# Correlation products on two 64-wide column tiles, with the high parts multiplied in one direction only

## The chip, the cores and the metric

One core of a Trainium2 chip. The metric is the device time of one execution in microseconds (us). One profiled execution gives the trace. Engines: PE multiplies matrices, DVE, ACT and POOL work on vectors, SP issues DMAs.

## The reference

Two layers with the same form are applied to x of shape (8, 512, 32, 32). Each normalizes x in 32 groups of 16 channels, correlates every pixel with its 5 x 5 neighbours (dot products over 512 channels of vectors of unit length), appends these 25 numbers to the channels, multiplies by a 512 x 537 matrix, adds a bias, applies relu and adds the result to x:

```python
norm = jnp.sqrt(jnp.sum(feature * feature, axis=1, keepdims=True))
fn = feature / jnp.maximum(norm, EPS)
fp = jnp.pad(fn, ((0, 0), (0, 0), (PAD, PAD), (PAD, PAD)))
sims = []
for cc in range(CS):
    for r in range(CS):
        sims.append(jnp.sum(fp[:, :, r:h + r, cc:w + cc] * fn, axis=1))
vol = jnp.stack(sims, axis=1)
x = jnp.concatenate([feature, vol], axis=1)
out = jnp.einsum('bihw,oi->bohw', x, conv_w) + conv_b[None, :, None, None]
return jax.nn.relu(out)
...
x = x + _L0_conv_ref(_gn(x), L0_conv_conv_w, L0_conv_conv_b)
x = x + _L1_conv_ref(_gn(x), L1_conv_conv_w, L1_conv_conv_b)
```

## The kernel before

A unit is one layer of one image; there are 16, in the order: layer 0 of images 0 to 3, layer 1 of the same, then images 4 to 7. A unit's x is four channel tiles of 128 channels (partitions) by 1024 pixels. The steps of unit u, and who does them:

- Statistics: DVE (`stats_tile`, L759; `stats_done`), PE averages them over groups (`average`, L461), DVE and ACT make scale and shift from that (`unit_affine`, L778 to L802; `deviations`, L621, the square root on ACT).
- Operands: ACT writes the normalized tile in f16, the high part (`norm_tile`, L627). ACT or, for units 0 to 2, POOL writes twice the exact value in f32 into `v2`, two buffers (`double_tile`, L633; `double_tiles`, L432). DVE subtracts twice the high part and so gets twice the low part in f16 (`low_tile`, L808).
- Correlation products (`product`, L470; `products`): the pixels are 8 blocks of 128 (4 image rows). For each block, PE multiplies the block's high part, as 128 weight columns, with high and with twice low of the 8 image rows around it: 256 columns, 192 at the image's edges. Four channel tiles accumulate. Two blocks share one bank of `gram_ps` (512 columns), and there are two banks, so the products of a unit are four steps p, and step p waits until ACT has evicted step p - 2 (`band_out_of_psum`, L643). Twice low, taken in one direction, stands for low in both, since the products of a pixel pair are later added up over both directions and halved.
- The band of products goes to DRAM and comes back skewed, so that each pixel has its neighbours in one row (`band_through_dram`, L340 and L346, on SP). DVE makes the vectors' lengths and scales (`neighbours`, L832 to L852), PE transposes (`turn`, L520), ACT copies the rows out (L654), SP writes them to DRAM (`rows_to_dram`, L356 and L358), POOL (SP for units 0 and 1) reads the shifted views back (`views_from_dram`, L267 to L277), DVE combines them (`correlation`, L817 to L825), and POOL moves the 25 numbers into `vol` (`volume_in`, L286).
- Channel products: 8 groups g of a unit (`channels`, L530), each 12 matmuls of 512 columns into one of four banks of `conv_ps`: high weights by high, low weights by high, and half the high weights (`whh`, made on POOL at L424) by twice low. `volume` (L539) adds the 25 numbers. ACT applies bias and relu (`rectified`, L662), DVE adds into x (`added`, L886).

All engines run their programs in the order in which they are written. From slot k = 3 on, a slot of PE is: products p = 0 and 1 of unit k, `average(k + 1)`, products 2 and 3, then groups 4 to 7 of unit k - 2 and 0 to 3 of unit k - 1, with `turn(k)` before the seventh. ACT evicts p = 0, takes the square root of unit k + 1, evicts p = 1, normalizes a tile of unit k + 1, and evicts p = 2 and 3. In slot 4 the weights of layer 1 are transposed between the groups (L510). SP loads images 4 to 7 in slots 4 and 6 to 8 (`load(TEAM)`, `tiles_in`), ahead of the rows of that slot.

Of the kernel before, what the change touches and what calls it, by code (L numbers as in the profile page):

```python
# [31 lines left out]
P = 128  # L32
# [25 lines left out]
def build(nc, x, w0, b0, w1, b1, out):  # L58
# [10 lines left out]
    BAND = (ROWS + 2 * R) * WI  # L69
    PAIRS = BLOCKS // 2  # L70
    REACH = 2 * R * WI + S
# [21 lines left out]
    GSZ = GPAD + BLOCKS * P * BAND + GPAD  # L93
    GROUPS = 2 * KT
    BN = 6
    assert (B, UNITS) == (BATCHES, B * LAYERS) and BAND * 2 == HALF
# [7 lines left out]
    with ctx:  # L104
# [17 lines left out]
        whh = sb("whh", [P, LAYERS, KT, C], F16)  # L122
# [3 lines left out]
        v2 = sb("v2", [P, 2, PIX], F32)  # L126
        band = sb("band", [P, PAIRS, HALF], F32)
# [19 lines left out]
        affine = sb("affine", [P, 2, 2, KT], F32)  # L147
# [30 lines left out]
        w_half = sem("w_half")  # L178
# [6 lines left out]
        twice = sem("twice")  # L185
        low = sem("low")
        gram = sem("gram")
# [16 lines left out]
        CONSTS = 11  # L204
        BN_STEPS = KT + KT + 2
        GN_STEPS = 11
# [41 lines left out]
        V2_ON_POOL = (0, 1, 2)  # L248
# [51 lines left out]
        def _(sp):  # L300
# [32 lines left out]
            def band_through_dram(k):  # L333

                q = k % 2
                for p in range(PAIRS):
                    sp.wait_ge(band_sb, PAIRS * k + p + 1)
                    dst = bass.AP(band_dram, q * GSZ + GPAD + 2 * p * P * BAND,
                                  [[BAND, P], [P * BAND, 2], [1, BAND]])
                    sp.dma_start(dst, band[:, p, :].rearrange("p (a n) -> p a n", a=2)).then_inc(band_out, 16)  # L340
                sp.wait_ge(band_out, 16 * PAIRS * (k + 1))
                wait(sp, rn_step, RN_STEPS * k)
                for h in range(HALVES):
                    src = bass.AP(band_dram, q * GSZ + GPAD - R + h * FOLD * P * BAND,
                                  [[BAND + 1, P], [P * BAND, FOLD], [1, REACH]])
                    sp.dma_start(skew[:, h:BLOCKS:HALVES, :], src).then_inc(skew_in, 16)  # L346
# [29 lines left out]
            for k in range(STEADY, SLOTS):  # L376
# [3 lines left out]
                tiles_out(k - 2, (2, 3))  # L380
                tiles_in(k - 2)
# [3 lines left out]
                if valid(k):  # L385
                    rows_to_dram(k)
# [5 lines left out]
        def _(pool):  # L392
# [14 lines left out]
            pool.memset(band[:, 0, 0:R * WI], 0.0).then_inc(const_step, 1)  # L407
            pool.memset(band[:, PAIRS - 1, HALF - R * WI:HALF], 0.0).then_inc(const_step, 1)
# [11 lines left out]
            def half_weights(l):  # L420

                for t in range(KT):
                    pool.wait_ge(w_high, W_HIGHS * l + t + 1)
                    pool.tensor_scalar(whh[:, l, t, :], wh[:, l, t, :], 0.5, 1.0, ALU.mult, ALU.mult  # L424
                                       ).then_inc(w_half, 1)

            def double_tiles(u, tiles):

                pool.wait_ge(gn_step, GN_STEPS * (u + 1))
                for t in tiles:  # L430
                    wait(pool, low, KT * u + t - 1)
                    pool.tensor_scalar(v2[:, t % 2, :], xs[:, ring_slot(unit_batch(u)), t, :],  # L432
                                       affine[:, 1, 0, t:t + 1], affine[:, 1, 1, t:t + 1], ALU.mult, ALU.add
                                       ).then_inc(twice, 1)

            double_tiles(0, range(KT))
            scaled_weights(0)
            half_weights(0)
            double_tiles(1, range(KT))
            volume_in(pool, 0)  # L440
            double_tiles(2, range(KT))
            volume_in(pool, 1)
            for k in range(EARLY, UNITS):
                if k == W1_SLOT:
                    half_weights(1)
# [7 lines left out]
        def _(pe):  # L453
# [10 lines left out]
            def product(u, j, t, part):  # L464

                p, h = j // 2, j % 2
                r0 = max(ROWS * j - R, 0)
                r1 = min(ROWS * (j + 1) + R, HI)
                at = h * BAND + (r0 - (ROWS * j - R)) * WI
                return pe.matmul(gram_at(u, p)[:, at:at + (r1 - r0) * WI],  # L470
# [519 lines left out]
```

## Time and profile before

| | |
|---|---|
| timed runs, us | 540.31, 537.4, 541.9 (median 540.31) |
| span of the profiled execution, us | 538.4 (its total is not given apart) |
| PE busy | 490.8 us, 91% of the span, 2824 matmuls |
| DVE, ACT, POOL busy | 350.5 (65%), 278.6 (52%), 131.8 (24%) |
| channel products L530, chain that ended last | 56% of the span |
| correlation products L470, same chain | 14% |
| moved by DMA | 75.81 MB, 141 GB/s |

Matmuls are pipelined: a matmul's duration includes a tail in which the next one already runs, so the distance between two starts, not the duration, is what one costs in a row. PEld is the load of a matmul's weights, which runs beside the matmul before it. A share of the whole span is an average over a start, a steady stretch and an end with different limits.

### The profile page before, as it was taken

The page shows a single profiled execution, that of the slowest core. Times are in us where ns is not written, and L with a number is a line of the kernel's source. Part 1 is how long each engine was busy: PE and PEld are TensorE (multiplying, and loading weights), DVE is VectorE, ACT ScalarE, POOL GpSimd, SP SyncE. Part 2 cuts the span into 40 slices and gives each one's busy share as a digit, 9 for nine tenths or more (in the row PEclk, how much of TensorE's full clock was granted, in tenths as well). Part 3 has the DMA queues.
Part 4 walks back from the last instruction along what each step waited for, and adds up shares of the span by engine and source line. Part 5 has one row for each costly group of instructions (what it writes and reads, how often), then busy time and mean ns, then how long its engine had stood idle before and what let it go on. Part 6 is the DMA issues. An engine that isn't in the chain of part 4 may idle for free.

```text
span 538.4 us, 7705 instructions
## 1 busy us (share of the span) xinstructions
PE 490.8 (91%) x2824; PEld 278.2 (52%) x2824; DVE 350.5 (65%) x820; ACT 278.6 (52%) x370; POOL 131.8 (24%) x189
## 2 busy tenths in 40 slices
PE   0658699489998999999999999999999999999996
PEld 0535355354644646464645556464646455564442
DVE  4788794767869296958758595858677676433322
ACT  1352544575394656647393757556473938433222
POOL 3453511040521313131220404040313112040400
PEclk9989799789999999999999999999999999999999
DMA  8282444441332716494957625042332326362332
GB/s 295 99 270 67 129 165 133 133 134 38 94 92 74 219 49 211 149 309 131 321 165 254 212 102 161 15 129 47 98 89 75 110 79 185 138 203 90 126 126 114
DMA packets 58547, 75.81 MB, mean 141 GB/s; under 512 B 11764, under 2 KB 45612, under 8 KB 58510
## 3 DMA queue, kind: packets, MB, share of 16 engines
q1 hardware_dynamic: 48718, 66.40, 36.7%
q0 software_dynamic: 9792, 8.92, 7.0%
q8 instruction: 22, 0.36, 0.3%
q14 instruction: 15, 0.12, 0.1%
HBM read 34.97 MB, written 37.79 MB: 135 GB/s over the span
## 4 chain that ended last, share of the span: by engine, by line
PE 77%; DVE 10%; ACT 4%; DMA 4%; POOL 2%; SPq 2%; issue 2%; DVEq 0%; ACTq 0%
PE conv_ps L530 56%; PE gram_ps L470 14%; PE conv_ps L539 5%; DVE stats L759 3%; POOL v L432 2%; DVE opnd L808 2%; DMA xs<-in_x_dram 1%; ACT opnd L627 1%; PE turn_ps L520 1%; ACT v L633 1%; DVE wmax L858 1%; ACT act_out L662 1%; DMA skew<-band_dram 1%; DMA band_dram<-band 1%; DVE xs L886 1%
## 5 line engine op out<-in xcount | busy, mean ns | idle before, releaser
L530 PE MATMUL conv_ps<-opnd,wh 128*128 128x512 f16 x512 | 194.9, 381 | 1.2 <-DVE wl L874 1.2
L530 PE MATMUL conv_ps<-opnd,whh 128*128 128x512 f16 x512 | 194.7, 380 | 0.0
L530 PE MATMUL conv_ps<-opnd,wl 128*128 128x512 f16 x512 | 194.7, 380 | 0.0
L662 ACT ACTIVATE act_out<-conv_ps,bias,wdown 128x512 f32<-128x512 f32 x128 | 96.4, 775 | 141.0 <-PE conv_ps L539 129.1
L886 DVE TENSOR_TENSOR xs<-xs,act_out 128x512 f32<-128x512 f32 x128 | 87.7, 696 | 50.8 <-ACT act_out L662 50.2
L470 PE MATMUL gram_ps<-opnd 128*128 128x256 f16 (+1 forms) x960 | 105.0, 269 | 3.4 <-ACT band L643 3.4
L470 PEld LDWEIGHTS gram_ps<-opnd 128*128 128x128 f16 x960 | 91.1, 100 | 16.6 <-ACT band L643 3.7
L808 DVE SCALAR_TENSOR_TENSOR opnd<-opnd,v 128x1024 f16<-128x1024 f16 x64 | 78.4, 1235 | 28.7 <-ACT v L633 21.3
L627 ACT ACTIVATE opnd<-xs,affine 128x1024 f16<-128x1024 f32 x64 | 78.8, 1238 | 17.4 <-DVE affine L802 17.4
L759 DVE BATCH_NORM_STATS2 stats<-xs 128x6 f32<-128x512 f32 x128 | 79.9, 681 | 5.6 <-DMA xs<-in_x_dram 5.6
L530 PEld LDWEIGHTS conv_ps<-opnd,whh 128*128 128x128 f16 x512 | 50.0, 98 | 61.2 <-issue 1.0
L530 PEld LDWEIGHTS conv_ps<-opnd,wh 128*128 128x128 f16 x512 | 50.2, 98 | 58.8 <-POOL whh L424 1.3
L530 PEld LDWEIGHTS conv_ps<-opnd,wl 128*128 128x128 f16 x512 | 50.2, 98 | 57.5 <-issue 0.8
L633 ACT ACTIVATE v<-xs,affine 128x1024 f32<-128x1024 f32 x52 | 64.4, 1238 | 6.1 <-DVE opnd L808 6.1
L267 POOL DMA_DIRECT2D mirror<-rows_dram x14 | 9.5, 678 | 232.0 <-DMA rows_dram<-rows 232.0
L286 POOL DMA_DIRECT2D vol<-corr_h x48 | 33.2, 697 | 105.7 <-DVE corr_h L825 105.6
L539 PE MATMUL conv_ps<-vol,wvol 96*128 96x512 f16 x128 | 47.2, 396 | 11.7 <-DMA vol<-corr_h 11.7
L643 ACT ACTIVATE band<-gram_ps 128x448 f32<-128x448 f32 (+1 forms) x60 | 32.5, 560 | 20.2 <-PE gram_ps L470 20.2
L817 DVE TENSOR_TENSOR mirror<-mirror,rn_own 100x256 f32<-100x256 f32 x16 | 6.8, 424 | 49.1 <-DMA rn_far<-rows_dram 49.1
L277 POOL DMA_DIRECT2D rn_far<-rows_dram x56 | 34.1, 744 | 0.0
L539 PEld LDWEIGHTS conv_ps<-vol,wvol 96*128 96x128 f16 x128 | 12.6, 100 | 27.6 <-DMA vol<-corr_h 12.3
L432 POOL TENSOR_SCALAR v<-xs,affine 128x1024 f32<-128x1024 f32 x12 | 21.7, 1817 | 18.5 <-DVE affine L802 11.8
(77 smaller groups left out, 238.6 us busy)
## 6 DMA issues: line engine op xcount, KB each, us to landing
xs<-in_x_dram SPq DMA_DIRECT2D x32, 512.0 KB, 6.4
band_dram<-band SPq DMA_DIRECT2D x64, 256.0 KB, 2.9
out_dram<-xs SPq DMA_DIRECT2D x32, 512.0 KB, 2.9
skew<-band_dram SPq DMA_DIRECT2D x32, 266.0 KB, 3.5
vol<-corr_h POOLq DMA_DIRECT2D x48, 50.0 KB, 2.7
rows_dram<-rows SPq DMA_DIRECT2D x32, 65.8 KB
rows_dram<-rows SPq DMA_DIRECT2D x32, 63.3 KB
mirror<-rows_dram POOLq DMA_DIRECT2D x14, 110.9 KB, 2.6
```

Source lines behind the costliest of these rows:

```text
L277: eng.dma_start(rn_far[c:QPARTS:QUARTERS, 0:run], bass.AP(rows_dram, rn_row + c * QRUN, [[1, S], [PW, S], [1, run]])).then_inc(arrived, 16)
L286: eng.dma_start(vol[at:at + NS, k % 2, :].rearrange("s (q n) -> s q n", q=QUARTERS), corr_h[:, part, :]).then_inc(vol_in, 16)
L470: return pe.matmul(gram_at(u, p)[:, at:at + (r1 - r0) * WI], opnd[:, u % RING, 0, t, j * P:(j + 1) * P], opnd[:, u % RING, part, t, r0 * W ...
L530: pe.matmul(conv_ps[:, g % 4, :], w[:, l, t, m * P:(m + 1) * P], opnd[:, u % RING, part, t, n * HALF:(n + 1) * HALF], start=(t == 0 and w ...
L539: pe.matmul(conv_ps[:, g % 4, :], wvol[0:96, l, m * P:(m + 1) * P], vol[0:96, u % 2, n * HALF:(n + 1) * HALF], start=False, stop=True).the ...
L627: act.activation(opnd[:, u % RING, 0, t, :], xs[:, ring_slot(unit_batch(u)), t, :], ACT.Identity, bias=affine[:, 0, 1, t:t + 1], scale=aff ...
L633: act.activation(v2[:, t % 2, :], xs[:, ring_slot(unit_batch(u)), t, :], ACT.Identity, bias=affine[:, 1, 1, t:t + 1], scale=affine[:, 1, 0 ...
L643: act.activation(band[:, p, a:z], gram_at(u, p)[:, a:z], ACT.Copy).then_inc(band_sb, 1)
L662: act.activation(act_out[:, g % 2, :], conv_ps[:, g % 4, :], ACT.Relu, bias=bias[:, l, m:m + 1], scale=wdown[:, l, m:m + 1]).then_inc(relu, 1)
L759: last = dve.bn_stats(stats[:, t, h, :], xs[:, ring_slot(b), t, h * HALF:(h + 1) * HALF])
L808: dve.scalar_tensor_tensor(out=opnd[:, u % RING, 1, t, :], in0=opnd[:, u % RING, 0, t, :], scalar=-2.0, in1=v2[:, t % 2, :], op0=ALU.mult, ...
L886: dve.tensor_tensor(xt, xt, act_out[:, g % 2, :], ALU.add).then_inc(x_sum, 1)
```

## The change

- The products work on 16 tiles of 2 image rows (64 pixels) in place of 8 blocks of 4. A tile's high part is 64 weight columns; the even tile of a block writes partitions 0 to 63 of the bank, the odd one 64 to 127, each on its own half of the array's columns (a column tile).
- Per tile and channel tile there are two products: high by low of the 6 rows around it (192 columns, low in both directions, no longer doubled), and high by `half`, a new buffer, of 128 columns: its own 2 rows halved and the 2 rows ahead in full. So the high parts are multiplied in one direction. A filler product opens the columns that lie off the image for the first and the last tile.
- DVE makes `half` with two instructions per channel tile (`half_tile`); there is one buffer, so they wait for the products of the unit before.
- v is the exact value, no longer doubled; the low part is a plain subtraction; `whh` and the POOL step that made it go, and so does DVE's step that doubled the affine numbers.
- A bank holds 2 x 192 columns in place of 512, of blocks p and p + 4; all of them are evicted. A band row is 384 contiguous numbers in DRAM; four DMAs in place of two read it skewed.
- SP issues the rows' DMAs before the loads of the next image.

```diff
-            def product(u, j, t, part):
...
+            def low_product(u, n, t):
+
+                above, below = off_image(n)
+                first, size = (TROWS * n - R) * WI + above, BAND - above - below
+                pe.matmul(tile_at(u, n, above, size), opnd[:, u % RING, 0, t, n * TILE:(n + 1) * TILE],
+                          opnd[:, u % RING, 1, t, first:first + size],
+                          start=(t == 0 and opens(u, n) and size == BAND), stop=False)
+
+            def high_product(u, n, t):
+
+                size = AHEAD if n < TILES - 1 else TILE
+                return pe.matmul(tile_at(u, n, R * WI, size), opnd[:, u % RING, 0, t, n * TILE:(n + 1) * TILE],
+                                 half[:, t, n, 0:size], start=False,
+                                 stop=(t == KT - 1 and (u > 0 or not opens(u, n))))
+
+            def block_products(u, j, t):
+
+                tiles = range(j * SPLIT, (j + 1) * SPLIT)
+                if t == 0:
+                    for n in tiles:
+                        filler(u, n)
+                for n in tiles:
+                    low_product(u, n, t)
+                for n in tiles:
+                    last = high_product(u, n, t)
+                return last
...
             def products(u, p):
 
                 if p == 0:
-                    pe.wait_ge(high, KT * (u + 1))
                     pe.wait_ge(low, KT * (u + 1))
+                    pe.wait_ge(halved, 2 * KT * (u + 1))
                 pe.wait_ge(band_sb, PAIRS * u + p - 1)
-                for j in (2 * p, 2 * p + 1):
+                for j in (p, p + FOLD):
                     for t in range(KT):
-                        for part in range(2):
-                            last = product(u, j, t, part)
+                        last = block_products(u, j, t)
                 last.then_inc(gram, 1)
...
-                    for w, part in ((wh, 0), (wl, 0), (whh, 1)):
+                    for w, part in ((wh, 0), (wl, 0), (wh, 1)):
...
-                a = R * WI if p == 0 else 0
-                z = HALF - (R * WI if p == PAIRS - 1 else 0)
-                act.activation(band[:, p, a:z], gram_at(u, p)[:, a:z], ACT.Copy).then_inc(band_sb, 1)
+                act.activation(band[:, p, :], gram_at(u, p)[:, 0:PITCH], ACT.Copy).then_inc(band_sb, 1)
...
-                dve.wait_ge(twice, KT * u + t + 1)
-                dve.scalar_tensor_tensor(out=opnd[:, u % RING, 1, t, :], in0=opnd[:, u % RING, 0, t, :], scalar=-2.0,
-                                         in1=v2[:, t % 2, :], op0=ALU.mult, op1=ALU.add).then_inc(low, 1)
+                dve.wait_ge(exact, KT * u + t + 1)
+                dve.tensor_tensor(opnd[:, u % RING, 1, t, :], v[:, t % 2, :], opnd[:, u % RING, 0, t, :], ALU.subtract
+                                  ).then_inc(low, 1)
+
+            def half_tile(u, t):
+
+                h = opnd[:, u % RING, 0, t, :].rearrange("p (n x) -> p n x", x=TILE)
+                wait(dve, gram, PAIRS * u)
+                dve.tensor_scalar(half[:, t, :, 0:TILE], h, 0.5, None, ALU.mult).then_inc(halved, 1)
+                dve.tensor_copy(half[:, t, 0:TILES - 1, TILE:AHEAD], h[:, 1:TILES, :]).then_inc(halved, 1)
...
                 tiles_out(k - 2, (2, 3))
+                if valid(k):
+                    rows_to_dram(k)
                 tiles_in(k - 2)
                 if k == W1_SLOT:
                     sp.wait_ge(w_turned, LAYERS * (KT + 1))
                     load(TEAM)
-                if valid(k):
-                    rows_to_dram(k)
```

On PE, the end of the products of unit 5, before the change (`gram_ps` is the bank of products, L461 the average):

```order
L461 MATMUL turn_ps<-mv,avg 128x8
L470 MATMUL gram_ps<-opnd 128x256 x24
L470 MATMUL gram_ps<-opnd 128x192 x8
L530 MATMUL conv_ps<-opnd,wh 128x512
L530 MATMUL conv_ps<-opnd,wl 128x512
```

The last block of the same products on PE after the change (L477 the filler, L485 the low products, L492 the high ones):

```order
L477 MATMUL gram_ps<-opnd 64x64
L485 MATMUL gram_ps<-opnd 64x192
L485 MATMUL gram_ps<-opnd 64x128
L492 MATMUL gram_ps<-half,opnd 64x128
L492 MATMUL gram_ps<-half,opnd 64x64
```

Where 32 products of 128 rows stood after the average, there are now 65 of 64 rows, and consecutive ones alternate between the two column tiles; the last block shown has the image's lower edge.

On DVE, in slot 4 before the change, from the tiles of unit 5 to the low weights of layer 1 (L808 low products' operand, L886 sum into x, L832 to L852 neighbours, L874 low weights):

```order
L808 SCALAR_TENSOR_TENSOR opnd<-opnd,v 128x1024
L886 TENSOR_TENSOR xs<-xs,act_out 128x512
L874 TENSOR_TENSOR wl<-gram_ps,wh 128x512
L886 TENSOR_TENSOR xs<-xs,act_out 128x512
L874 TENSOR_TENSOR wl<-gram_ps,wh 128x512
```

The same place on DVE after the change (L831 the operand, L838 and L839 the two instructions of `half_tile`, L916 the sum, L904 the low weights):

```order
L831 TENSOR_TENSOR opnd<-v,opnd 128x1024
L838 TENSOR_SCALAR half<-opnd 128x16x64
L839 COPY half<-opnd 128x15x64
L916 TENSOR_TENSOR xs<-xs,act_out 128x512
L904 TENSOR_TENSOR wl<-gram_ps,wh 128x512
L916 TENSOR_TENSOR xs<-xs,act_out 128x512
L904 TENSOR_TENSOR wl<-gram_ps,wh 128x512
```

Two instructions now stand between the unit's last operand tile and the sum, and so ahead of the low weights too; six more of their kind stand earlier in the slot.

## Rows read from the trace of the kernel before

**Rows 1.** Busy time of each engine by stretch of the span, with the clock.

```profile
core 0: us, PE busy (x) PEld busy (x) DVE busy (x) ACT busy (x) POOL busy (x), PEclk, DMA share, GB/s
...
77.08:104.37 27.29, 20.10 (x125) 12.24 (x124) 16.57 (x44) 14.25 (x18) 2.08 (x3) 0.89 0.46 132
104.37:138.46 34.09, 31.90 (x175) 18.19 (x174) 26.17 (x64) 18.97 (x25) 6.36 (x10) 0.94 0.29 81
138.46:173.87 35.41, 32.23 (x195) 18.79 (x193) 27.82 (x54) 20.58 (x29) 12.86 (x18) 1.00 0.27 79
173.87:470.40 296.53, 296.53 (x1742) 167.54 (x1742) 201.87 (x492) 176.40 (x230) 63.48 (x100) 1.00 0.47 148
470.40:538.40 68.00, 63.30 (x329) 31.73 (x327) 19.90 (x39) 19.12 (x27) 12.69 (x20) 1.00 0.39 134
```

**Rows 2.** Timeline of PE, products of one unit: start us, us, engine, line, operation, count.

```profile
203.52 3.44 PE L470 MATMUL gram_ps<-opnd 128*128 128x192 f16 x32
...
207.20 3.46 PE L470 MATMUL gram_ps<-opnd 128*128 128x256 f16 x32
210.50 0.38 PE L530 MATMUL conv_ps<-opnd,wh 128*128 128x512 f16 x1
```

**Rows 3.** Timeline of PE: narrow transposes, then the 128-wide average.

```profile
33.74 0.49 PE L510 MATMUL conv_ps<-ident,opnd 128*25 128x128 f32 x3
...
34.06 0.29 PE L461 MATMUL turn_ps<-mv,avg 128*128 128x8 f32 x2
```

**Rows 4.** Groups by line and shape: weight loads; busy us, mean ns | idle before, releaser.

```profile
L470 PEld LDWEIGHTS gram_ps<-opnd 128*128 128x128 f16 x960 | 91.1, 100 | 16.6 <-ACT band L643 3.7 <-DVE wvol L878 0.4
...
L520 PEld LDWEIGHTS turn_ps<-ident,nbr 128*115 128x115 f32 x64 | 9.5, 187 | 6.5 <-DVE nbr L852 4.2 <-issue 0.3
...
L510 PE MATMUL conv_ps<-ident,opnd 128*25 128x128 f32 x4 | 0.6, 272 | 0.0
...
L510 PEld LDWEIGHTS conv_ps<-ident,opnd 128*25 128x25 f32 x4 | 0.4, 104 | 0.0
```

**Rows 5.** Timeline of all engines: from the average to the eviction of p = 1.

```profile
325.53 0.29 PE L461 MATMUL turn_ps<-mv,avg 128*128 128x8 f32 x2
...
326.65 0.21 ACT L621 ACTIVATE gstd<-gvar 128x4 f32<-128x4 f32 x1 [2.12 <-DVE gvar L785]
326.76 0.58 ACT L643 ACTIVATE band<-gram_ps 128x512 f32<-128x512 f32 x1
```

**Rows 6.** Groups by line and shape: DVE and ACT.

```profile
L808 DVE SCALAR_TENSOR_TENSOR opnd<-opnd,v 128x1024 f16<-128x1024 f16 x64 | 78.4, 1235 | 28.7 <-ACT v L633 21.3 <-POOL v L432 7.2
...
L643 ACT ACTIVATE band<-gram_ps 128x512 f32<-128x512 f32 x30 | 17.4, 580 | 3.6 <-PE gram_ps L470 3.6
...
L820 DVE TENSOR_TENSOR corr<-own,mirror 100x256 f32<-100x256 f32 x16 | 6.8, 425 | 0.5
...
L823 DVE TENSOR_SCALAR corr_h<-corr 100x256 f16<-100x256 f32 x16 | 4.7, 294 | 0.6
```

**Rows 7.** The chain that ended last, in order of time: start us, us, what.

```profile
101.06 1.23 DVE opnd L808
...
110.59 5.12 PE gram_ps L470 x32
...
162.63 0.61 DVE wl L874
...
163.38 0.63 PE gram_ps L510 x4
```

**Rows 8.** DMA issues: queue, operation, count, KB each, us from issue to landing.

```profile
xs<-in_x_dram SPq DMA_DIRECT2D x32, 512.0 KB, 6.4
...
skew<-band_dram SPq DMA_DIRECT2D x32, 266.0 KB, 3.5
```

More of the change, by code:

```diff
@@ L125, in build @@
         vol = sb("vol", [P, 2, PIX], F16)
-        v2 = sb("v2", [P, 2, PIX], F32)
-        band = sb("band", [P, PAIRS, HALF], F32)
+        v = sb("v", [P, 2, PIX], F32)
+        half = sb("half", [P, KT, TILES, AHEAD], F16)
+        band = sb("band", [P, PAIRS, PITCH], F32)
         skew = sb("skew", [P, BLOCKS, REACH], F32)
@@ L418, in scaled_weights, with exact_tiles @@
                                        ALU.mult, ALU.mult).then_inc(w_scaled, 1)
[L420 to L427, printed above, removed]
+            def exact_tiles(u, tiles):
                 pool.wait_ge(gn_step, GN_STEPS * (u + 1))
@@ L462, in average, with off_image @@
                           start=True, stop=True).then_inc(group_avg, 1)
-            def product(u, j, t, part):
[L466 to L470, printed above, removed]
-                                 opnd[:, u % RING, 0, t, j * P:(j + 1) * P],
-                                 opnd[:, u % RING, part, t, r0 * WI:r1 * WI],
-                                 start=(t == 0 and part == 0 and (u > 0 or h == 0)),
-                                 stop=(t == KT - 1 and part == 1 and (u > 0 or h == 1)))
+            def off_image(n):
+                top = TROWS * n - R
+                return max(-top, 0) * WI, max(top + TROWS + 2 * R - HI, 0) * WI
@@ new lines, in tile_at, with opens, filler @@
+            def tile_at(u, n, first, size):
+                j, s = n // SPLIT, n % SPLIT
+                at = j // FOLD * BAND + first
+                return gram_at(u, j % FOLD)[s * TILE:(s + 1) * TILE, at:at + size]
+            def opens(u, n):
+                return u > 0 or n // SPLIT < FOLD
+            def filler(u, n):
+                above, below = off_image(n)
+                if above or below:
+                    size = above + below
+                    pe.matmul(tile_at(u, n, 0 if above else BAND - below, size),
+                              opnd[:, u % RING, 0, 0, n * TILE:(n + 1) * TILE],
+                              opnd[:, u % RING, 0, 0, 0:size], start=opens(u, n), stop=False)
@@ L480, in first_products @@
                     pe.wait_ge(low, t + 1)
+                    pe.wait_ge(halved, 2 * (t + 1))
                     for p in range(PAIRS):
-                        for j in (2 * p, 2 * p + 1):
-                            for part in range(2):
-                                last = product(0, j, t, part)
+                        for j in (p, p + FOLD):
+                            last = block_products(0, j, t)
                         if t == KT - 1:
@@ L918, in _ @@
             low_tile(2, 2)
+            half_tile(2, 2)
             neighbours(1)
```

107 lines of the change are left out of this document (56 added, 51 removed).

## The prediction

> **What bounds the kernel now.** I read the busy time by stretch first. From 173.87 to 470.40, which is ten slots of 29.65 us (units 5 to 14), TensorE (PE) is busy 296.53 of 296.53 us at a granted clock of 1.00, while DVE is busy 201.87 and ACT 176.40 [rows 1]. There nothing but TensorE's own work counts. The three slots before it are different: PE is busy 20.1 of 27.3, 31.9 of 34.1 and 32.2 of 35.4 us, DVE up to 79% [rows 1]; there PE waits for chains that run through DVE. After 470.40 PE is busy 63.30 of 68.00 us.
>
> Next I read PE's timeline at the head of a slot. The correlation products of one unit begin at 203.52, the second half at 207.20, and the first channel product follows at 210.50 [rows 2]: 6.98 us of 29.65. The second half is 32 matmuls with 24 x 256 + 8 x 192 = 7680 columns in 3.30 us, 0.43 ns a column; their weight loads hide under the matmuls.
>
> **The products.** Before, a unit has 64 products over 15360 columns. After, each of 8 blocks has, per channel tile, two low products of 192 columns (one per column tile) and two high products of 128, 64-wide in weights; the edges are 64 columns shorter and get two small fillers. By the 0.43 ns a column, a 192 takes 82 ns and a 128 takes 55 ns [rows 2]. If the two column tiles run beside each other, one block and channel tile costs 82 + 55 = 137 ns; if not, 275 ns. Before it was two matmuls of 256, about 220 ns. Call this period T; a unit has 32 of them: 4.4 or 8.8 us.
>
> The trace of before has no two tiles that overlap, so both ends stay in the range. I take the lower one, with 5 ns for filling, T = 142: the tiles use different array columns and different partitions of the bank, the loop alternates between them, and a narrow tile is seen to load its next weights under its running matmul: the 25-column weights start three matmuls in 0.49 us each 0.27 long, so 0.11 apart, with loads of 0.10 that cost nothing [rows 3, 4].
>
> What may spoil it is the weight load. Every product has its own, so there are four per period instead of two. Between the 25 and the 115 columns of f32 the load grows from 104 to 187 ns, 0.92 ns a column; 128 columns of f16 take 98 to 100 ns [rows 4]. If an f16 column costs half of an f32 one, 64 of them occupy 29 ns, four 118, which hides under T. At the f32 price they occupy 59, four of them 236, and T would be the loads. That is a rival below.
>
> Here the Trainium skill speaks against the change: "TensorEngine Tiling (Array Packing)", Restrictions, says that column tiling disables the fast weight load, and "TensorE: Matmul & The Clock Gate", LDWEIGHTS, gives columns / 1.2 ns, 53 ns for 64. By that four loads take 213 ns, and T would be 213, the phase 7.1 us, +1 in all, the start +7: 548 us in place of 525. No run here shows an f16 load of 64 columns.
>
> **The wait that comes in its place.** The order on PE is products p0, p1, average(k+1), p2, p3. p3 reuses p1's bank, and ACT evicts p1 only after the square root of deviations(k+1), which needs the average through four DVE steps: from the average at 325.53 to the end of that eviction at 326.76 + 0.58 = 327.34 it is 1.81 us [rows 5]. Before, p2 (1.65 us) hid nearly all of it. Now p2 takes 8 T = 1.14 us. The eviction is 384 columns in place of 512, between 0.44 (in proportion) and 0.58 [rows 6]; with 0.50 the chain is 1.73. So p3 starts 1.75 us after p1's end and 0.4 us of PE are idle. The phase becomes 16 T + 1.75 + 8 T = 2.27 + 1.75 + 1.14 = 5.16 us, 1.82 less than 6.98. Eleven slots (units 5 to 15) have it: -20.0 us. Without that new wait it would be 2.2 x 11 = 24.
>
> **DVE's halving.** Each channel tile gets two more f16 instructions on DVE, of 1024 and 960 elements. From 425 ns at 256 elements and 1235 at 1024, one element costs 1.05 ns and the rest 155; the TENSOR_SCALAR of 256 took 294, so 0.54 an element with a 4-byte source [rows 6]. At that rate the two take 0.71 + 0.67; if it is bytes that count, half of that a column, 0.43 + 0.41. I take 0.8 us per tile and keep 1.4 as the other end; one per cycle would be 2.4. In the bound stretch 4 x 0.8 = 3.2 us a unit go on DVE's 20.2 a slot: 23.4 of 27.8, hidden. Each halving also waits for all products of the unit before; these end 7 us into a slot [rows 2], and DVE comes to the first halving after two low products, later than that. Behind it on DVE stand the sums into x, which ACT and then PE's four banks wait for; four banks of (29.65 - 6.98) / 8 = 2.8 us each cover 0.8. The subtraction that replaces the old low product has the same element count and two sources: nothing.
>
> In the start nothing hides them. (a) For units 0 and 1 the last tile's halving stands between the low products and the next work on DVE: 1.6 us. (b) For unit 2 I count three of four: 2.4. (c) For unit 3, two halvings stand after neighbours(2) and before the low product that is on the chain at 101.06, two more before the statistics whose average holds p2 at 110.59 [rows 7]: 2.0 of 3.2 net of ACT's own time. The shorter products give 2 back in that slot. (d) In slot 4 halvings stand ahead of the low weights at 162.63, which PE waits for at 163.38 [rows 7]: 1.0. Together +5.0, with ends 0 (all in DVE's idle time, products' gain kept) and +12 (1.4 a tile).
>
> **Edits at nothing.** The halved weights go from POOL; PE's first wait then falls on the low weights, which end at the same time. The doubled affine step (128x8) goes from DVE. The band's DRAM pieces keep their bytes but the two skew reads become four: two more issues on SP, where one lands in 3.5 us [rows 8], in a chain that PE meets only six groups later. SP issues the rows' four DMAs ahead of the four input loads; a load of 512 KB lands 6.4 us after its issue [rows 8], and its statistics stand a slot later, so lateness is covered; what the loads now collide with is the views' reads. If that cover failed on the four slots that have loads, it is 4 x 6.4 = 26 us; if the earlier rows help, the start gains 1 to 3. I take nothing.
>
> **Sum.** The profile gives a span of 538.4 and no total of its own; the three timed runs are 537.4 to 541.9, median 540.31, so 1.9 is added to the span. 538.4 + 1.9 + 5.0 - 20.0 = 525.3, say 525 us.
>
> **Rivals.**
> 1. The weight loads set T (59 ns each, 236): the phase is 32 T + 0.25 = 7.8 us, +0.8 x 11 = +9, and the start keeps +7 without the products' return: 556. Halfway (43 ns each, T = 172): 16 T + 1.75 + 8 T = 5.9, -1.1 x 11 = -12, +5.5: 534. For it: nothing in the trace has a load rate for plain f16. Against: the loads shown start with the matmul before, far ahead of need. 545 is its middle. Chance 0.18.
> 2. The other side: the column tiles don't overlap. Each stream then waits for the one before, T = 275, the phase is 8.8 + 0.25 - 0.2 for the edges = 8.9, +1.9 x 11 = +21, start +8: 569. It decides as soon as T passes 210, where 32 T + 0.25 equals the old 6.98. For it: no overlap of two matmuls' streams is seen anywhere, their starts are always a full stream apart [rows 2, 3]. Against: it would need the engine to treat two disjoint halves as one. That is also the case in which the change does not do what it says. Chance 0.14.
> 3. The engine empties when the tile width changes, four times a unit (into and out of the products, and around the average). A tail is 0.27 - 0.11 = 0.16 us [rows 3, 4], four are 0.65, x 11 = 7: 532. The trace is against it: 25-wide matmuls at 33.74 are followed by the 128-wide average at 34.06, 0.32 = 3 x 0.107 later [rows 3]. The Trainium skill, "TensorEngine Tiling (Array Packing)", Tiling Modes, says that changing the mode drains the engine; the trace does not agree, with those 0.32 us. Chance 0.06.
> 4. DVE's halving runs one element per cycle, 2.4 us a tile: 20.2 + 9.6 = 29.8 a slot, and with DVE's waits it becomes the bound: about +2 x 11 + 15: 575 or more. Against: the TENSOR_SCALAR row. Chance 0.04.
> The forecast has 0.58, with its own range 517 to 534.
>
> **How the numbers follow.** A measurement of this kernel tells about 1% from no change, 534.9 to 545.7. Faster: 0.55 of the forecast (0.03 of it goes to the slow halving, 1.4 a tile, at about 530 to 537), 0.05 of rival 3, 0.02 of rival 1: 0.62. Slower: rivals 2 and 4, 0.18, and 0.07 of rival 1: 0.25. The same: the rest, 0.13. The range goes from 517 (T = 137, start at 0 or better) to 563, which cuts through rival 2.
>
> **What the profile after would show.** Right: slots 27.8 us apart in a stretch where PE is still near 100%; the products' phase 5.2 us; a pair of tiles starting within 30 ns; PE idle 0.4 us a slot before the last quarter of the products, released by ACT's band; two half instructions of about 0.4 us; slot 5 starting near 179 in place of 173.87. Wrong: starts of the products 70 ns or more apart on average (each alone), 64-column loads with PE waiting behind them, or DVE at the bound.

## The result, and the profile after

The changed kernel takes 548.03 us (median of 4 runs, 546.84 to 550.23) where the kernel before takes 540.56 (4 runs, 537.4 to 541.9): a ratio of 1.0152 (95% interval 1.0126 to 1.0177). It is slower by 1.5%, where 525 and a gain were forecast. The profiled execution has a span of 545.1 us against 538.4, so the trace shows a difference of 6.7 us.

Where it lies is seen in the busy time by stretch of the changed kernel. The columns are those of [rows 1], and the cuts are the starts of slots 5, 10 and 15, which in the kernel before are at 173.9, 322.2 and 470.4:

```profile
108.60:144.10 35.50, 32.39 (x240) 19.47 (x240) 31.00 (x73) 18.17 (x24) 6.36 (x10) 0.83 0.25 69
144.10:180.00 35.90, 32.26 (x263) 17.88 (x262) 30.64 (x63) 20.44 (x29) 9.29 (x14) 0.95 0.23 66
180.00:335.00 155.00, 145.60 (x1201) 77.30 (x1200) 115.13 (x280) 86.55 (x114) 32.17 (x50) 0.98 0.56 179
335.00:479.20 144.20, 141.09 (x1203) 76.59 (x1204) 118.16 (x283) 87.58 (x116) 31.98 (x50) 1.00 0.36 96
479.20:545.10 65.90, 61.23 (x395) 30.12 (x394) 19.82 (x39) 18.68 (x27) 12.66 (x20) 0.99 0.39 134
```

| us | before | after | difference |
|---|---|---|---|
| start, to slot 5 | 173.9 | 180.0 | +6.1 |
| slots 5 to 9 | 148.3 | 155.0 | +6.7 |
| slots 10 to 14 | 148.1 | 144.2 | -3.9 |
| from slot 15 on | 68.0 | 65.9 | -2.1 |

[Rows 1] had one stretch with PE busy throughout; after the change it is two. In slots 10 to 14 the change gains. In slots 5 to 9, in which images are loaded and stored (179 GB/s against 96), PE stands idle for 9.4 us and the stretch is longer than before.

The products themselves do what they should. Timeline of PE at the head of slot 14, for [rows 2, 3]:

```profile
450.41 0.38 PE L569 MATMUL conv_ps<-vol,wvol 96*128 96x512 f16 x1
450.72 0.22 PE L477 MATMUL gram_ps<-opnd 128*64 128x64 f16 x1
...
453.06 0.39 PE L454 MATMUL turn_ps<-mv,avg 128*128 128x8 f32 x2
453.38 0.27 PE L485 MATMUL gram_ps<-opnd 128*64 128x192 f16 x2
453.48 0.22 PE L492 MATMUL gram_ps<-half,opnd 128*64 128x128 f16 x2
453.54 0.25 PE L485 MATMUL gram_ps<-opnd 128*64 128x192 f16 x2
453.62 0.22 PE L492 MATMUL gram_ps<-half,opnd 128*64 128x128 f16 x2
453.68 0.25 PE L485 MATMUL gram_ps<-opnd 128*64 128x192 f16 x2
...
454.92 0.27 PE L485 MATMUL gram_ps<-opnd 128*64 128x192 f16 x2 [0.24 <-ACT band L668]
...
456.14 0.39 PE L560 MATMUL conv_ps<-opnd,wh 128*128 128x512 f16 x1
```

Each row has both column tiles (x2), and a period of a low and a high pair is 0.14 us (453.54 to 453.68), as if one tile ran alone. PE waits 0.24 us before the last quarter. The phase is 450.72 to 456.14 = 5.42 us.

The groups by line and shape answer to [rows 4, 6]:

```profile
L485 PE MATMUL gram_ps<-opnd 128*64 128x192 f16 x840 | 77.4, 260 | 6.9 <-ACT band L668 6.9
...
L485 PEld LDWEIGHTS gram_ps<-opnd 128*64 128x64 f16 x960 | 65.1, 116 | 9.3 <-ACT band L668 9.1
...
L839 DVE COPY half<-opnd 128x960 f16<-128x960 f16 x64 | 41.4, 646 | 0.0
L838 DVE TENSOR_SCALAR half<-opnd 128x1024 f16<-128x1024 f16 x64 | 27.0, 422 | 0.0
...
L668 ACT ACTIVATE band<-gram_ps 128x384 f32<-128x384 f32 x60 | 27.7, 479 | 15.4 <-PE gram_ps L492 15.4
```

A weight load of 64 columns lasts 116 ns, longer than that of 128 [rows 4], but a period of 0.14 us leaves no time in which PE could wait for one. The halving takes 422 ns as chosen; the copy 646.

What holds slots 5 to 9 is in the chain that ended last. One turn of it, in slots 7 and 8 (start us, us, what):

```profile
252.53 0.42 DVE mirror L847
...
254.46 2.36 DVE opnd L831 x2
...
258.04 0.56 DVE half L839
...
261.84 0.09 DVE nsq L862
...
266.17 0.61 DVE xs L916
...
267.54 0.77 ACT act_out L687
268.31 0.51 ACT rows L679
268.83 0.34 SPq L361
...
270.51 2.45 DMA rows_dram<-rows
...
276.77 8.54 DMA rn_far<-rows_dram
285.33 0.43 DVE mirror L847
```

No long row of it is PE's. DVE combines the rows of one unit (L847), does its in-order work of the slot (low parts, halvings, sums, scales), ACT copies the next rows out behind its evictions, the rows go through DRAM, and DVE, which has stood idle 8 us, combines them: 252.53 to 285.33 = 32.8 us, where PE needs 28.4. The halvings in the loop are four tiles at 0.9 = 3.6 us.

How much room the loop had is seen in the same slots of the kernel before (L817 combines the rows, L852 is the end of `neighbours`, L520 `turn`, L654 the rows' copy):

```profile
243.13 0.43 DVE L817 TENSOR_TENSOR mirror<-mirror,rn_own 100x256 f32<-100x256 f32 x1 [3.70 <-DMA rn_far<-rows_dram]
...
252.06 0.90 DVE L852 TENSOR_TENSOR nbr<-skew,nbr 128x200 f32<-128x200 f32 x2
...
256.96 0.60 PE L520 MATMUL turn_ps<-ident,nbr 128*115 128x128 f32 x4
...
258.29 0.60 ACT L654 ACTIVATE rows<-turn_ps 115x512 f32<-115x512 f32 x1
...
274.24 0.42 DVE L817 TENSOR_TENSOR mirror<-mirror,rn_own 100x256 f32<-100x256 f32 x1 [5.17 <-DMA rn_far<-rows_dram]
```

This turn takes 31.1 us and the next one 30.0, but the distance of two starts is not the loop's own length: where PE sets the slots, every step comes back after one slot on average. In each turn the loop itself waits for PE: 4.0 us from the end of `neighbours` (252.96) to `turn` (256.96), and 2.9 in the next turn. Without that wait both turns are 27.1 us, so the room was 2.5 us to PE's 29.6. After the change the wait is 0.05 us (264.14 to 264.19), and PE waits for `neighbours` instead. Against the first of these turns, 1.8 us are added before the end of `neighbours`, 2.7 between `turn` and the rows' copy (4.0 in place of 1.3, since ACT's evictions there wait for DVE's sums) and 1.2 in the rows' way through DRAM: from 27.1 to 32.8.

PE meets DVE's late work in two places. Its waits in slots 5 to 9 of the changed kernel (total us, times, longest; L550 is `turn`, L454 the average):

```profile
PE turn_ps L550 <- DVE nbr L882: 5.3, 3, 2.1
PE turn_ps L454 <- DVE mv L797: 2.6, 4, 1.9
PE gram_ps L485 <- ACT band L668: 1.4, 5, 0.3
```

The same view of the kernel before shows none in these slots. Beside the waits, the same matmuls keep PE busy for 145.6 us here and for 141.1 in slots 10 to 14; the clock fell twice here (last section).

### The profile page after: what moved, and what is told of

It reads as the page before. It is cut to its first block, busy times and chain, and to the rows that moved or that the text cites. A ratio compares the mean times of both kernels' runs of the same rounds, so it can differ in the third digit from the quotient of the medians.

```text
span 545.1 us, 9949 instructions
## 1 busy us (share of the span) xinstructions
PE 478.3 (88%) x3880; PEld 262.4 (48%) x3880; DVE 402.3 (74%) x932; ACT 274.6 (50%) x370; POOL 119.5 (22%) x179
## 3 DMA queue, kind: packets, MB, share of 16 engines
q1 hardware_dynamic: 41038, 62.21, 35.3%
## 4 chain that ended last, share of the span: by engine, by line
PE 41%; DVE 32%; DMA 11%; ACT 5%; issue 5%; POOL 4%; SPq 2%; DVEq 0%; ACTq 0%
PE conv_ps L560 33%; DVE opnd L831 7%; DMA rn_far<-rows_dram 7%; DVE stats L784 5%; DVE half L839 4%; DVE xs L916 4%; PE gram_ps L485 3%; PE conv_ps L569 3%; DVE half L838 2%; DMA rows_dram<-rows 2%; ACT act_out L687 2%; DMA xs<-in_x_dram 1%; POOL rn_far L282 1%; DVE nbr L882 1%; PE gram_ps L492 1%
## 5 line engine op out<-in xcount | busy, mean ns | idle before, releaser
L560 PE MATMUL conv_ps<-opnd,wh 128*128 128x512 f16 x1024 | 329.0, 386 | 0.9 <-DVE wl L904 0.9
L560 PEld LDWEIGHTS conv_ps<-opnd,wh 128*128 128x128 f16 x1024 | 101.5, 99 | 125.1 <-issue 8.4
L916 DVE TENSOR_TENSOR xs<-xs,act_out 128x512 f32<-128x512 f32 x128 | 87.0, 692 | 32.9 <-ACT act_out L687 32.7
L831 DVE TENSOR_TENSOR opnd<-v,opnd 128x1024 f16<-128x1024 f32 x64 | 81.0, 1275 | 14.2 <-ACT v L660 11.0
L654 ACT ACTIVATE opnd<-xs,affine 128x1024 f16<-128x1024 f32 x64 | 78.9, 1238 | 15.6 <-DVE affine L824 15.6
L485 PE MATMUL gram_ps<-opnd 128*64 128x192 f16 x960 | 77.4, 256 | 6.9 <-ACT band L668 6.9
L492 PE MATMUL gram_ps<-half,opnd 128*64 128x128 f16 x960 | 75.5, 227 | 0.0
L485 PEld LDWEIGHTS gram_ps<-opnd 128*64 128x64 f16 x960 | 65.1, 116 | 9.3 <-ACT band L668 9.1
L492 PEld LDWEIGHTS gram_ps<-half,opnd 128*64 128x64 f16 x960 | 65.4, 117 | 0.0
L847 DVE TENSOR_TENSOR mirror<-mirror,rn_own 100x256 f32<-100x256 f32 x16 | 6.8, 423 | 56.1 <-DMA rn_far<-rows_dram 56.1
L839 DVE COPY half<-opnd 128x960 f16<-128x960 f16 x64 | 41.4, 646 | 0.0
L668 ACT ACTIVATE band<-gram_ps 128x384 f32<-128x384 f32 x60 | 27.7, 479 | 15.4 <-PE gram_ps L492 15.4
L838 DVE TENSOR_SCALAR half<-opnd 128x1024 f16<-128x1024 f16 x64 | 27.0, 422 | 0.0
```

Source lines behind the costliest of these rows:

```text
L485: pe.matmul(tile_at(u, n, above, size), opnd[:, u % RING, 0, t, n * TILE:(n + 1) * TILE], opnd[:, u % RING, 1, t, first:first + size], sta ...
L492: return pe.matmul(tile_at(u, n, R * WI, size), opnd[:, u % RING, 0, t, n * TILE:(n + 1) * TILE], half[:, t, n, 0:size], start=False, stop ...
L560: pe.matmul(conv_ps[:, g % 4, :], w[:, l, t, m * P:(m + 1) * P], opnd[:, u % RING, part, t, n * HALF:(n + 1) * HALF], start=(t == 0 and w ...
L654: act.activation(opnd[:, u % RING, 0, t, :], xs[:, ring_slot(unit_batch(u)), t, :], ACT.Identity, bias=affine[:, 1, t:t + 1], scale=affine ...
L831: dve.tensor_tensor(opnd[:, u % RING, 1, t, :], v[:, t % 2, :], opnd[:, u % RING, 0, t, :], ALU.subtract).then_inc(low, 1)
L839: dve.tensor_copy(half[:, t, 0:TILES - 1, TILE:AHEAD], h[:, 1:TILES, :]).then_inc(halved, 1)
```

## The experiments

Theory L: DVE's added instructions lengthen this loop, and in the slots with loads the loop, not PE, sets the period. The rivals: the loads' new place alone does it (C), the amount of DVE's work alone (D, A), or only waits worth themselves. "Slots 5 to 9" is read from the starts of the products in each profile. In the expectations TensorE, VectorE and ScalarE are PE, DVE and ACT.

**1. The loads' place.** The changed kernel with the loads ahead of the rows again:

```diff
+                tiles_in(k - 2)
                 if valid(k):
                     rows_to_dram(k)
-                tiles_in(k - 2)
```

> The changed kernel with SP's old order: the input loads ahead of the rows. Theory L: slots 5 to 9 (180.0 to 335.0, 155 us for five) are set by a loop, correlation(k-1) to low tiles and halvings to neighbours(k) to turn(k) to rows to views to correlation(k), 32.8 us in the slots with loads (252.5 to 285.3); the loads lengthen only its part from the rows' issue to the correlation (16.4 us against 13.8 to 15.3 before), so about 1.5 us on three or four slots come back: 542 to 543 us. Rival C (the loads' collision alone makes slots 5 to 9 long): all 13 us over 28.4 each come back, 535. Rival D (DVE simply has too much work): nothing, 548.

554.22 us, ratio 1.0255 (1.0214 to 1.0296):

```profile
182.20:343.30 161.10, 148.34 (x1201) 78.70 (x1200) 115.28 (x280) 86.41 (x114) 32.10 (x50) 0.96 0.53 171
```

None of the three had it: L and C expected a gain and D nothing, but the new place helps by 6 us. Slots 5 to 9 take 161.1, and the difference is in slot 5 (35.3 us against 28.8); slots 6 to 9 take 125.8 against 126.2. And the kernel before with only the rows moved ahead of the loads:

> The kernel before with nothing but the rows' DMAs ahead of the input loads. Theory L: its loop without halvings is about 30 us with loads, near its 29.6 us slot, so 1.5 us longer from rows to correlation shows in part: 540.5 to 543. Rival C: the collision costs by itself, 13 us less the new slot's 1.2 x 5: about 547. If the order helps: under 540.

538.91 us, ratio 0.9986 (0.9969 to 1.0004): nothing, with slots 5 to 9 at 148.1. So the move alone costs nothing where the loop has room, and rival C is out.

**2. The halvings behind `neighbours`.**

```diff
-                    half_tile(k + 1, 0)
-                    half_tile(k + 1, 1)
...
-                        half_tile(k + 1, j + 1)
+                    if j == 3 and valid(k + 1):
+                        for t in range(KT):
+                            half_tile(k + 1, t)
```

> The changed kernel with all four halvings of a slot moved on DVE from before and around neighbours(k) to behind it (from slot 3 on); the same instructions, the loads still behind the rows. Theory L: three halvings of 0.9 us leave the loop, which goes from 32.8 to about 30.1 us in the slots with loads; three slots gain 2.7 each, one or two gain less: 539 to 541. Rival C (collision alone) and rival D (too much work on DVE): nothing, 548.

558.0 us, ratio 1.035 (1.0315 to 1.0385): a miss for all three. The lengths came earlier, but the sums, and with them ACT's evictions and the rows, came later (in slots 7 to 9 the rows' copy began 6.5 to 6.6 us after `turn` began, where it was 4.0), and PE's waits for the average grew to 37.1 us in 12, from 22.1 in 8 over the whole span. The loop passes DVE's in-order work up to the sums that ACT needs before the rows; a step moved inside it stays in it.

**3. A faster copy, and no copy.** The same 960 elements in two even halves, of 15 x 32 each:

```diff
-                dve.tensor_copy(half[:, t, 0:TILES - 1, TILE:AHEAD], h[:, 1:TILES, :]).then_inc(halved, 1)
+                two = lambda a: a.rearrange("p n (a x) -> p a n x", a=2)
+                dve.tensor_copy(two(half[:, t, 0:TILES - 1, TILE:AHEAD]), two(h[:, 1:TILES, :])).then_inc(halved, 1)
```

> The changed kernel with the second halving instruction written with its 32-column halves as the outermost dimension (2 in place of 15), same elements. If the odd 15 is what makes it slow, it goes from 646 to about 420 ns: 0.22 x 3 = 0.7 us per turn of the loop and about 0.2 to 0.9 per unit at the start, 544 to 546 us by theory L. If not, 646 ns stay and 548. By rival C the slots with loads don't gain.

541.39 us, ratio 1.0039 (1.0014 to 1.0065). The two instructions in its groups:

```profile
L838 DVE TENSOR_SCALAR half<-opnd 128x1024 f16<-128x1024 f16 x64 | 30.3, 473 | 0.0
L840 DVE COPY half<-opnd 128x960 f16<-128x960 f16 x64 | 25.6, 400 | 0.0
```

The pair went from 1068 to 873 ns, 0.8 us a unit, and the kernel gained 6.6, more than the 2 to 4 expected. In the profiled executions, which differ by 8.4, it is 3.0 at the start and 5.2 in slots 5 to 9 (149.8). Then all copies from unit 3 on were left out:

> The changed kernel without the copies of units 3 to 15 (highs of the rows ahead are then those of unit 2, so the results are not the reference's); TensorE's instructions are the same. Theory L: 2.6 us of in-order work less per unit take the loop from 32.8 to about 30 us, slots 5 to 9 from 155.0 to 143 to 147 us: 538 us (535 to 541). Rival F (VectorE's work is hidden in these slots): 548.

535.80 us, ratio 0.9928 (0.9906 to 0.9951), slots 5 to 9 at 147.3, near what L said. With PE's instructions unchanged, 2.6 us of DVE a unit decide over 12 us.

**4. The DVE part alone.** The kernel before, with the halving and the copy into a buffer that nobody reads, behind each low part:

```diff
+            def half_tile(u, t):
+                h = opnd[:, u % RING, 0, t, :].rearrange("p (n x) -> p n x", x=64)
+                wait(dve, halved, 2 * (KT * u + t))
+                dve.tensor_scalar(half[:, :, 0:64], h, 0.5, None, ALU.mult).then_inc(halved, 1)
+                dve.tensor_copy(half[:, 0:15, 64:128], h[:, 1:16, :]).then_inc(halved, 1)
...
                 low_tile(0, t)
+                half_tile(0, t)
...
```

> The kernel before with the two VectorE instructions of each tile (halving and copy, 0.42 and 0.65 us) added behind each low part, into a buffer that nobody reads; TensorE's work is the old one. Theory L: 4.3 us of in-order work more per unit make the loop of the slots with loads about 32 to 33 us where TensorE needs 29.6: some 10 us in slots 5 to 9, and 5 to 6 us at the start: 555 us (550 to 560). Rival F (VectorE's added work is hidden in the slots that TensorE fills, only the start shows it): 546.

561.88 us, ratio 1.0413 (1.0387 to 1.0439): +22, past the 550 to 560 that L gave. Busy time of its slots 5 to 9 and 10 to 14:

```profile
182.90:343.90 161.00, 152.79 (x871) 84.28 (x871) 116.49 (x285) 87.91 (x114) 31.68 (x50) 0.98 0.54 179
343.90:493.20 149.30, 148.38 (x872) 83.77 (x871) 120.23 (x289) 89.04 (x116) 32.06 (x50) 1.00 0.34 101
```

By the profiled spans the DVE part costs 9.0 at the start, 12.7 in slots 5 to 9 and 1.2 in slots 10 to 14; rival F had nothing for the slots, and its 6 us for the start were too few. From here to the changed kernel 2.6 points of the ratio come back, 14 us, in two steps. The changed kernel with the loads ahead of the rows (experiment 1) has this kernel's DVE work and order of the loads, and the new products: it is 1.6 points faster, 8 us, nearly all of it in slots 10 to 14 (149.3 to 144.2) and behind them (68.0 to 65.9). Slots 5 to 9 stay as they are, 161.0 and 161.1: the loop sets them, so a shorter products' phase gives nothing there. The other 6 us are the rows' new place.

**5. The bytes of the loads.** Everything issued, but 64 columns instead of 1024 for images 5 to 7:

```diff
-                        sp.dma_start(xs[:, ring_slot(b), t, :], x_v[b, :, t, :]).then_inc(x_in[ring_slot(b)][t], 16)
+                        sp.dma_start(xs[:, ring_slot(b), t, 0:64], x_v[b, :, t, 0:64]).then_inc(x_in[ring_slot(b)][t], 16)
```

> The changed kernel with the loads that SP issues for images 5 to 7 cut from 1024 to 64 columns, so the results of these images are not the reference's; all instructions and waits stay. Theory L with the loads' bytes as what lengthens the way of the rows: issue to correlation falls from 16 to about 11 us in the slots with loads, the loop from 32.8 to about 28, slots 6 to 9 come to 28.4 to 29 us: 538 us (535 to 541). Rival A (VectorE's added work alone makes the loop too long): 547.

536.3 us, ratio 0.9928 (0.9906 to 0.995): as L said. From the end of the rows' copy in slots 6 and 7 to the correlation it is now 13.1 us, where it was 16.4 and 16.5. The loads' bytes are the other part of the loop, and with them gone DVE's work nearly fits. Taking either part out brings back about 12 us, so neither alone is "the" cause.

**6. The order on ACT.** Evictions of pairs 0 and 1 ahead of the square root, to remove the wait of 0.24 us:

```diff
                     band_out_of_psum(k, 0)
+                    band_out_of_psum(k, 1)
                     if valid(k + 1):
                         deviations(k + 1)
-                    band_out_of_psum(k, 1)
-                    if valid(k + 1):
                         norm_tile(k + 1, 0)
```

> The changed kernel with ScalarE's evictions of pairs 0 and 1 ahead of the square root and of the first tile of the next unit. The wait of TensorE before pair 3 (0.25 us, 12 times) goes. Theory L: it is worth something only in the slots in which the loop does not set the period (10 to 15): 0.25 x 6 to 9 = about 2 us, 546.5. Rival A (each wait is worth itself): 545. Rival N (the first tile comes 0.5 us later and VectorE with it, which the loop passes on): 549.

549.99 us, ratio 1.019 (1.016 to 1.022), which overlaps that of the changed kernel: at best nothing. Quiet slots fell to 28.0 us, but slots 5 to 9 rose to 157.3. Rival N is the nearest.

**7. Correlation later on DVE, alone and with others.**

```diff
-                if valid(k - 1):
-                    correlation(k - 1)
                 if valid(k + 1):
                     low_tile(k + 1, 0)
                     low_tile(k + 1, 1)
                     half_tile(k + 1, 0)
                     half_tile(k + 1, 1)
+                if valid(k - 1):
+                    correlation(k - 1)
```

> The changed kernel with correlation(k-1) on VectorE placed behind the low parts and halvings of tiles 0 and 1 instead of ahead of them. Theory L (a loop from correlation over VectorE's in-order work to the rows and back through DRAM sets the period of slots 5 to 9): VectorE stood 7.9 us for rn_far in slot 7, and 4.6 us of tile work fits into that, so the loop falls from 32.8 to about 28.4 us, slots 5 to 9 from 155.0 to 143 to 148 us: 539 us (536 to 543). Rival A (VectorE's amount of work, not its order, is what counts): 548. Rival V (the volume's images, sent 4 us later, become late for TensorE): slower than 550.

550.14 us, ratio 1.0203 (1.0151 to 1.0256): a miss for L. DVE's wait for the rows was gone in these slots, but the period of slots 7 to 9 stayed at 32 us. In the profiled execution (554.2, the longest of the four) slots 5 to 9 gained 1.4 us, while slot 5 began at 184.9 in place of 180.0, and slots 10 to 14 rose from 144.2 to 148.0, since PE waits for the average there. Its chain shows what took the place:

```profile
281.82 0.83 ACT band L668 x2
...
282.66 7.61 DMA band_dram<-band
...
290.28 0.64 SPq L351
...
292.87 4.67 DMA skew<-band_dram
297.57 0.18 DVE nsq L862
```

The band's write, 3 us as a rule, takes 7.6 here behind the loads, and DVE waits for the skewed bands instead (nsq, the first step of `neighbours`). Followed further, the chain goes over DVE's sums and statistics, the average and the scales to ACT and back to the band, 32.7 us a turn (277.0 to 309.7). There are two loops, one by the rows and one by the bands; the loads issued behind the rows lie across both. With the faster copy and the order of 6 added:

> The changed kernel with three edits: the copy in two even halves (541.4 alone), correlation behind tiles 0 and 1, and ScalarE's first two band evictions ahead of the square root. Theory L: 541.4 less 5 for the order of the correlation and less 2 for the 0.25 us per slot before pair 3: 534 us (531 to 538), under the kernel before. Rival A (amount of VectorE work only): 539.

540.98 us, ratio 1.0011 (0.9988 to 1.0035): a miss, no more than the copy alone gives. Slots 5 to 9 came to 145.6, but slot 5 began at 181.1 instead of 177.0 with the copy alone.

**8. The loads between the two.** With the faster copy, SP issues the loads when DVE has read the skewed bands, ahead of the rows:

```diff
+                if valid(k) and valid(k - 2) and unit_layer(k - 2) == 1:
+                    sp.wait_ge(rn_step, RN_STEPS * k + 1)
+                tiles_in(k - 2)
                 if valid(k):
                     rows_to_dram(k)
-                tiles_in(k - 2)
```

> The changed kernel with the copy in two even halves (541.4 alone) and SP's loads of images 5 to 7 issued when VectorE has read the skewed bands, ahead of the rows, so that they fall into the stretch of some 6 us between the landing of skew and the issue of the rows. Theory L: the loads' bytes lengthen the way of the rows from 11 to 16 us, here by half of that; slots 5 to 9 fall from 149.9 to 143 to 146 us: 536 us (533 to 538). Rival A (loads ahead of the rows delay the rows as in the run with loads first, +6): 547.

543.54 us, ratio 1.0059 (1.0036 to 1.0083): a miss. The rows now come behind the loads: 15.0 and 14.7 us from issue to the correlation in slots 7 and 8, but the issue waits 2 us for the four loads, so that it is 17.0 and 16.7 from the end of the rows' copy, where the copy alone has 16.2 and 16.0. Slots 5 to 9 take 152.0. Then the same with correlation later (7) and the evictions first (6), both from slot 5 on only:

> The run before this one with two more edits that hold from slot 5 on: correlation behind tiles 0 and 1, and the evictions of pairs 0 and 1 ahead of the square root. Theory L: with a shorter loop TensorE sets the slots, the evictions take 0.35 us from each slot without a load as in the run that had them alone (28.4 to 28.0) and the start is kept: 534 us (531 to 537), under the kernel before. Rival N (the first tile comes later and the way of the bands takes the place of the way of the rows): 539.

528.66 us, ratio 0.9792 (0.9766 to 0.9817): faster than both kernels, and than L's 531 to 537. Its slots 5 to 9 and 10 to 14:

```profile
179.00:321.30 142.30, 140.23 (x1201) 76.50 (x1200) 113.07 (x282) 87.23 (x115) 34.19 (x50) 1.00 0.60 196
321.30:463.50 142.20, 140.42 (x1203) 76.55 (x1202) 112.36 (x281) 87.34 (x115) 34.54 (x50) 1.00 0.33 94
```

Slots with loads are now like those without. As I read it, the band has a free way, the late correlation covers the rows' longer one, and the copy shortens DVE's part; the three weren't taken apart further. The quiet slots stayed at 28.4, not the 28.0 expected: in place of PE's wait for the band stands one of 0.35 us for the average (1.1 once, in slot 8), whose statistics stand behind the late correlation. The start still has its +5.1 (179.0 to 173.9). Whether the kernel before would gain from the same orders wasn't tried; its slots 5 to 14 are PE's 29.6 already.

## Why the prediction was wrong

- **The step that failed** is "DVE's halving ... 23.4 of 27.8, hidden". It compared DVE's work with the length of a slot. In slots 5 to 9 of the kernel before, 26.4 us of DVE's idle time are five waits for rows whose way begins at DVE's own earlier work; in slots 10 to 14 these are 8.4 (total us, times, longest):

```profile
DVE mirror L817 <- DMA rn_far<-rows_dram: 26.4, 5, 7.9
...
DVE mirror L817 <- DMA rn_far<-rows_dram: 8.4, 5, 4.3
```

New work ahead of the rows doesn't fill such a wait, it pushes it along. The loop had 2.5 us of room in slots 7 and 8, and the change adds 5.6, of which 4.5 are ahead of the rows. The prediction did ask what later sums hold up, and found that PE's four banks cover it; it didn't ask about the rows, which ACT copies behind the same evictions (4.0 us after `turn` begins, before 1.3). Forecast for the whole DVE part: +5; measured alone, in the old order of the loads: +22 (experiment 4). Without loads the step held: slots 10 to 14 cost 1.2 us there.
- **The products' gain was counted in eleven slots** ("There nothing but TensorE's own work counts"). With the loop in charge, slots 5 to 9 have none of it (161.0 and 161.1, experiment 4).
- **The size of the copy** was the smaller error: 0.41 expected, 646 ns found. As durations the pair is 1.07 us, in a row 0.9 (0.34 + 0.56 in the chain), where 0.8 was chosen and 1.4 kept as the other end. With the copy at 400 ns, near the forecast's, the kernel still ties with the one before (experiment 3). Rival 4 had the engine right but the mechanism wrong: DVE is never full (115 of 155 us).
- **The loads' order at nothing**: it gives 6 us in the changed kernel and nothing in the kernel before (experiment 1). "Its statistics stand a slot later, so lateness is covered" looks only at whether the loads come late. What their bytes hold up are the rows and bands, and with the bytes gone 12 us come back (experiment 5).
- **The products' period**, T = 142 ns, was right (139 to 142), and rivals 1 and 2 fell. The Trainium skill had been cited against this: "TensorEngine Tiling (Array Packing)", Restrictions, on the fast weight load, and "TensorE: Matmul & The Clock Gate", LDWEIGHTS, for the price of a load. The estimate worked out from that price is a period of 213 ns and a phase of 7.1 us, and the measured 139 to 142 ns and 5.42 us disagree. That the same estimate ends at 548 us, the measured time, is chance. The measured time also lies inside the stated 517 to 563, but the upper part of that range stood for rival 2, so this is luck too.
- **The gain per slot** was over-sized: 29.61 to 28.44 us in quiet slots, 1.2, not 1.82. Three parts: the old phase is 6.70 to 6.74 in nine of the ten slots, and the slot shown in [rows 2] has a wait in it (0.28); the new phase is 5.42, not 5.16 (0.26); the step from the slot before into it is 0.31 instead of 0.22 (0.09). Ten slots at 1.2 and a last phase shorter by 2.1 would make 14. The changed kernel has only 8 of it (experiment 4). The last run of experiment 8, where the loop is short enough everywhere, has all of it: 296.4 to 284.5 us in slots 5 to 14, and the 2.1.
- **Rival 3**, the engine emptying at a change of tile width, was to cost 0.65 us a slot; at most 0.27 is seen. The distances at the four changes in slot 14 are 0.312, 0.149, 0.185 and 0.152 us, where the kernel before has 0.220, 0.109, 0.112 and 0.082: 0.27 more in all. Whether the engine empties there isn't shown by a run of its own, but the reading of [rows 3] as evidence against it was too strong.
- **The new wait** of PE came where and because of what was said, 0.24 us for 0.4. The start came at +6.1 for +5.0; its parts (a) to (d) weren't measured one by one, and the DVE part alone cost 9.0 there (experiment 4).

In sum: the products' -20.0 became -8, the DVE part's +5.0 became +22, and the 0 for the order of the loads became -6: +8 where -15 was forecast.

## What to carry to other kernels

An engine with idle time has room only if its idle time isn't a wait on its own earlier work. Follow the chain once round, take off what in it waits for the engine that sets the slot (here 4.0 and 2.9 us at `turn`), and compare the rest with the slot: 27.1 to 29.6 us was the room here, and neither the busy share nor the 4 to 8 us of one wait of DVE shows it. The distance between two starts of a step doesn't show it either, since in a steady stretch that is the slot, whoever sets it. A shorter phase on the engine that set the slot takes its gain from this room too. When two such loops run side by side, freeing one may show nothing; look which transfer lies across both. Here the loads' place, the order on DVE and ACT and the faster copy helped together, where experiments with part of them did not get below the kernel before.

## What was not expected of the hardware

- One copy of 960 f16 elements took 646 ns as 15 runs of 64 and 400 as two halves of 15 x 32. The Trainium skill, "VectorE: DVE Perf Modes", Mode 2×_2P, asks for an outermost dimension that is even, or odd and equal on both sides; both sides of the slow copy are written as 15 x 64, but the source's 960 elements lie in one run; if it counts as one run, which no run shows, the two durations agree with that rule. The halving beside it rose from 422 to 473 ns, for which no run gives a reason.
- PE's granted clock fell to its lower level (1.2 of 2.4 GHz) behind two waits in slots 5 to 9: behind the 2.03 us before `turn` in slot 7, and behind the 2.14 us before it in slot 8. Busy time by stretch of the changed kernel, with the granted clock third from the end:

```profile
262.00:264.00 2.00, 0.16 (x1) 0.00 (x0) 1.64 (x7) 1.49 (x3) 0.00 (x0) 1.00 0.64 262
264.00:266.00 2.00, 1.81 (x7) 1.19 (x8) 2.00 (x4) 0.00 (x0) 0.00 (x0) 0.57 0.00 0
266.00:269.00 3.00, 3.00 (x12) 1.18 (x11) 3.00 (x6) 1.94 (x3) 0.00 (x0) 0.72 0.26 106
269.00:272.00 3.00, 3.00 (x15) 1.26 (x13) 3.00 (x6) 0.78 (x1) 0.00 (x0) 1.00 0.42 140
...
298.40:301.80 3.40, 3.40 (x10) 1.20 (x9) 3.40 (x7) 1.94 (x3) 0.00 (x0) 0.50 0.23 95
```

From 264 to 269 the clock is 0.57 and 0.72, and 512-column matmuls start up to 0.43 us apart instead of 0.216. So a wait can cost more than itself. The fall does not follow from the wait's length alone: in the run with the correlation later (experiment 7) the clock fell behind a wait of 1.86 us at 277.9, and not behind one as long at 310.5.
